# Cross attention and a routed feed-forward layer on one core: token groups with the residual added on TensorE, the weight work moved

## What is computed

```python
q  = layernorm(x) @ Wq.T + bq            # then scores over the 64 keys
x  = x + softmax(q @ (ctx @ Wk.T).T * D**-0.5) @ (ctx @ Wv.T + bv) @ Wo.T + bo
xt = layernorm(x)
p, idx = top_k(softmax(xt @ Wr + br), 2);  p = p / p.sum()
h  = layernorm(relu(xt @ W1[e] + b1[e])) * g1[e] + be1[e]     # 128 -> 512
y  = layernorm(relu(h @ W2[e] + b2[e])) * g2[e] + be2[e]      # 512 -> 128
out = x + sum over the token's 2 experts of p * y
```

## Time and profile before

| | us |
|---|---|
| median of 3 runs | 352.91 (352.75 to 356.93) |
| profiled execution, its own time | 354.07 |
| span of its trace | 352.3 |
| busy: DVE, PE, ACT, POOL | 274.4 (78%), 226.2 (64%), 214.7 (61%), 172.8 (49%) |

### The profile page before, as it was taken

How to read it: one execution, slowest core, us unless ns; L and a number is a source line. 1 busy time by engine, 2 the same in 40 slices (tenths; PEclk the granted TensorE clock), 3 DMA queues, 4 the chain that set the end, 5 groups by cost and what they waited for, 6 DMA issues and landing times.

```text
span 352.3 us, 10394 instructions
## 1 busy us (share of the span) xinstructions
PE 226.2 (64%) x2809; PEld 188.6 (54%) x2809; DVE 274.4 (78%) x1263; ACT 214.7 (61%) x715; POOL 172.8 (49%) x265
## 2 busy tenths in 40 slices
PE   2960394956281402000299999999999989996900
PEld 2640343444141301000299999999999979982300
DVE  1885066548697987896069999999999989995396
ACT  2631092925446637231169999999999979984243
POOL 9001917443544736457005666666666656665000
PEclk9995558585555555555599999999999999996555
DMA  7798801110101101013121222222222222211964
GB/s 196 232 297 199 241 3 53 32 38 16 45 23 38 39 31 53 23 38 105 47 62 41 72 70 72 64 77 65 78 69 71 71 64 64 73 39 38 339 227 150
DMA packets 31278, 31.31 MB, mean 89 GB/s; under 512 B 5027, under 2 KB 23811, under 8 KB 31220
## 3 DMA queue, kind: packets, MB, share of 16 engines
q1 hardware_dynamic: 23716, 19.46, 19.9%
q0 software_dynamic: 4320, 8.89, 8.1%
q10 hardware_dynamic: 3184, 2.30, 2.0%
HBM read 18.66 MB, written 11.97 MB: 87 GB/s over the span
## 4 chain that ended last, share of the span: by engine, by line
PE 44%; DVE 25%; SPq 10%; issue 9%; another core or an unknown queue 3%; POOL 3%; DMA 3%; ACT 1%; DVEq 0%; ACTq 0%; POOLq 0%
PE bank L523 22%; PE bank L527 20%; SPq L393 4%; SPq L386 3%; PE bank L708 2%; POOL slot_rows L498 2%; DVE w2f L1270 2%; DVE x L1132 2%; DVE topi L1189 2%; DVE w2l L1276 2%; DVE w1l L1281 2%; DVE st L1139 1%; DVE w1f L1498 1%; DMA gb<-in_L_ffn_be 1%
## 5 line engine op out<-in xcount | busy, mean ns | idle before, releaser
L498 POOL DMA_INDIRECT slot_rows<-pay,pos x64 | 63.3, 990 | 61.0 <-DVE pos L1227 36.3
L510 POOL DMA_INDIRECT answers<-vo,xs x71 | 73.8, 1040 | 29.1 <-ACT sd L980 26.3
L523 PE MATMUL bank<-xsT,w1h 128*128 128x128 f16 x568 | 56.3, 221 | 0.7 <-issue 0.5
L1421 DVE SCALAR_TENSOR_TENSOR kb<-bank,rh 128x512 f16<-128x512 f32 x71 | 47.9, 675 | 10.9 <-ACT rh L966 10.8
L523 PE MATMUL bank<-xsT,w1l 128*128 128x128 f16 x284 | 52.2, 221 | 0.0
L527 PE MATMUL bank<-rh 128*128 128x129 f16 x284 | 51.5, 220 | 0.0
L527 PE MATMUL bank<-w2h,rh 128*128 x284 | 51.4, 219 | 0.0
L527 PE MATMUL bank<-w2l,rh 128*128 x284 | 51.4, 219 | 0.0
L966 ACT ACTIVATE rh<-bank 128x512 f16<-128x512 f32 x71 | 42.4, 597 | 14.4 <-PE bank L523 9.1
L523 PEld LDWEIGHTS bank<-xsT,w1h 128*128 x568 | 43.1, 99 | 3.6 <-issue 1.5
L527 PE MATMUL bank<-w2h,kb 128*128 x284 | 39.7, 220 | 1.3 <-DVE kb L1421 1.3
(11 more groups left out here) (212 smaller groups left out, 624.1 us busy)
## 6 DMA issues: line engine op xcount, KB each, us to landing
xs<-slot_rows SPq DMA_DIRECT2D x71, 64.5 KB
x_tok<-in_x SPq DMA_DIRECT2D x16, 128.0 KB, 3.0
w1f<-in_L_ffn_W SPq DMA_DIRECT2D x2, 1024.0 KB, 7.1
w1f<-answers SPq DMA_DIRECT2D x4, 512.0 KB, 5.1
w2f<-answers SPq DMA_DIRECT2D x4, 512.0 KB, 8.9
answers<-vo,xs POOLq DMA_INDIRECT x71
w2h<-in_L_ffn_W SPq DMA_DIRECT2D x4, 256.0 KB, 8.7
w2l<-in_L_ffn_W SPq DMA_DIRECT2D x4, 256.0 KB, 12.8
```

Source lines behind the costliest of these rows:

```text
L498: eng.indirect_dma_start(slots, bass.IndirectOffsetOnAxis(ap=pos[:, g % 2, k, i:i + 1], axis=0), pay[g % 2][:, k, i, :], None).then_inc(s_ ...
L510: eng.indirect_dma_start(answers, bass.IndirectOffsetOnAxis(ap=xs[j % NX][:, 2 * D:2 * D + 2].bitcast(U32), axis=0), z[j % NZ], None).then ...
L523: return eng.matmul(dst, lhsT, rhs, start=start, stop=stop)
L1421: eng.scalar_tensor_tensor(out=rl[j % 2][:, :, :], in0=psH[j % 3][:, :].rearrange("p (c n) -> p c n", c=FC), scalar=0.0, in1=rh_all(j), op ...
```

## The change

- x is loaded in 8 pieces with 1 KB runs; `w1_last` goes to ACT's DMA queue, g1, be1 and b2 are loaded ahead of W2, half of x behind W1.
- The residual and its router product are added by PE in the attention's PSUM bank (`skip`, 4 products of 136 columns); ACT copies the sum out (`x2_copy`) in place of DVE's `x2_`.
- The key bias enters PSUM as a product (8 or 24 rows by 256 columns) of the standard deviations' transpose and a table that POOL makes with 16 selects; DVE takes the maximum from PSUM, ACT's exponential scales by rstd. The probabilities are divided by their sum on DVE before the transpose.
- The root's guess is one exponential of the bits on ACT, then two Newton steps on DVE (6 steps for 12).
- Ranks are summed in PSUM over the groups (`base`, `ranks`, `base_next`); DVE's rank, count and cast instructions go.
- The copy of the payload is a DMA on SP instead of an ACT instruction.
- Orders: PE transposes x for group n+2 behind the ranks of group n-1, not ahead of the scores; ACT copies that transpose ahead of `xt`. Square sums go to passes 2 to 4 in quarters, centring to passes 4 to 7, the high parts to 6 to 8, and of the low parts 14 of 16 behind `tables`.

```diff
-        CENTRE = {3: (0, 1), 4: (2, 3), 5: (4, 5), 6: (6, 7)}
-        UP_LO = {5: (0,), 6: (1, 2), 7: (3, 4), 8: (5, 6, 7)}
-        DOWN_LO = {5: (0,), 6: (1, 2), 7: (3, 4), 8: (5, 6, 7)}
+        CENTRE = {4: (0, 1), 5: (2, 3), 6: (4, 5), 7: (6, 7)}
+        UP_LO = {7: (0, 1), 8: (2, 3, 4, 5, 6, 7)}
+        DOWN_LO = {8: range(8)}
...
+            for g in range(GROUPS):
+                eng.wait_ge(s_lo, g + 1)
+                eng.dma_start(pay[g % 2][:, 1, :, 0:2 * D], pay[g % 2][:, 0, :, 0:2 * D]).then_inc(s_copy[g % 2], 16)
...
+                mm(bank[1][:, 0:GT * KEYS], sdT[n][:, :],
+                   kb_tile[n][:, g * GT - first:(g + 1) * GT - first, :].rearrange("p i k -> p (i k)"), stop=False)
...
+            def skip(g):
+                if g >= 1:
+                    eng.wait_ge(s_x2, g)
                 for i in range(GT):
+                    mm_beside(attn(i // 2, i % 2), xT[g % 2][:, i * P:(i + 1) * P], ident_wr[:, :], i % 2 == 0)
...
+            def base_next(g):
+                m = mask[g % 2]
+                eng.wait_ge(s_pos, g + 1)
+                mm_beside(base, not_below[:, :], m[:, :])
+                for d in range(1, GT):
+                    t = mm_beside(base[:, 0:(GT - d) * E], onesb[:, :], m[:, d * E:])
...
+            def root_guess(v, y_, sem):
+                eng.activation(y_, v.bitcast(U32), ACT.Exp, bias=guess0[:, 0:1], scale=-0.5 * LN2 / (1 << MANTISSA)
+                               ).then_inc(sem, 1)
...
+            for e_ in range(E):
+                eng.dma_start(w1_last[e_], A["L0_ffn_W1"][e_, D - 1:D, :].to_broadcast([P, F])).then_inc(ld_w1_last, 16)
...
             tables()
+            for e_ in UP_LO[GROUPS]:
+                w_up_lo(e_)
+            for e_ in DOWN_LO[GROUPS]:
+                w_down_lo(e_)
             gate_diff()
             gates()
```

More of the change, by code:

```diff
@@ L163, in build @@
         oh = sb("oh", [P, GROUPS, K, GT, E])
-        mask = sb("mask", [P, GT, E], BF16)
-        filled = sb("filled", [P, 2, E])
-        rank = sb("rank", [P, GT, E])
-        pick = sb("pick", [P, K, GT, E])
-        posf = sb("posf", [P, K, GT])
+        mask = [sb(f"mask{n}", [P, GT * E], BF16) for n in range(2)]
+        pick = sb("pick", [P, K, GT * E])
         pos = sb("pos", [P, 2, K, GT], U32)
@@ L481, in gpsimd @@
                               channel_multiplier=0).then_inc(s_const, 1)
+            for n in range(2):
+                c, first = (FIRST, 0) if n == 0 else (TILES - FIRST, FIRST)
+                from_act(eng, f"key_bias{n}")
+                for b in range(c // 2):
+                    of_tile = kb[0:c, first // 2 + b:first // 2 + b + 1, :].to_broadcast([c, 2, KEYS])
+                    t = eng.affine_select(out=kb_tile[n][:, 2 * b:2 * b + 2, :], in_=of_tile, compare_op=ALU.is_equal,
+                                          fill=0.0, base=-2 * b, pattern=[[-1, 2], [0, KEYS]], channel_multiplier=1)
+                t.then_inc(s_sel, 1)
             eng.wait_ge(ld_w1_last, 16 * E)
@@ L603, in totals, with w_rows @@
                 mm(bank[6][:, 0:2 * FC + 1], ones[:, :], ss[:, :]).then_inc(p_tot, 1)
-            def w_rows(h):
-                eng.wait_ge(ld_b2, 16)
-                eng.wait_ge(s_gm, 1)
-                eng.wait_ge(ld_w2[h], 16)
-                mm(bank[6 + h][0:2, :], second[:, :], half(b2row, h), stop=False)
-                for n in range(h * H * FC, (h + 1) * H * FC):
+            def w_rows(h, part):
+                first = h * H * FC
+                if part == 0:
+                    eng.wait_ge(ld_b2, 16)
+                    eng.wait_ge(s_gm, 1)
+                    eng.wait_ge(ld_w2[h], 16)
+                    from_act(eng, "values2")
+                    mm(bank[6 + h][0:2, :], second[:, :], half(b2row, h), stop=False)
+                for n in range(first + part * H * FC // 2, first + (part + 1) * H * FC // 2):
                     at_d = (n // FC) % H * D
@@ L1093, in stats1, with newton @@
                 stat.up(t)
-            def root1_(first, end):
-                tiles = slice(first * GT, end * GT)
-                eng.wait_ge(q_stat, stat.n)
-                for k in range(12):
-                    root_step(k, 0, mv1a[:, tiles, 1], tiles, root1)
-            def bias_(g):
+            def newton(k, v, y_, yy, vyy, z, r):
+                a = y_ if k < 3 else z
+                if k % 3 == 0:
+                    return eng.tensor_tensor(yy, a, a, ALU.mult)
+                if k % 3 == 1:
+                    return eng.scalar_tensor_tensor(out=vyy, in0=yy, scalar=-0.5, in1=v, op0=ALU.mult, op1=ALU.mult)
+                return eng.scalar_tensor_tensor(out=z if k == 2 else r, in0=vyy, scalar=1.5, in1=a, op0=ALU.add,
+                                                op1=ALU.mult)
```

670 lines of the change are left out of this document (364 added, 306 removed).

## The result

| | kernel before | changed kernel |
|---|---|---|
| median of 4 runs, us | 353.33 (352.75 to 356.93) | 361.2 (359.63 to 364.1) |
| ratio, 95% interval | | 1.021 (1.011 to 1.031) |
| profiled execution: its time, span | 354.07, 352.3 | 359.9, 358.0 |

The change makes the kernel some 2% slower; the interval leaves out no change and reaches from 1 to 3%. I had forecast 341, 3% faster, with a range of 330 to 352: wrong in the direction, and outside the range.

What follows compares the result with a forecast made beforehand. It took the experts as bound by PE and the group loop by DVE and its waits. 19.7 us gained in the groups less 8.0 lost before the experts gave -11.7, so 341 us, range 330 to 352.

Steps and rivals of the forecast that it cites:

- The gain in the groups: Group loop: the last row numbers would end at 137.3 us against 157.0, 19.7 gained.
- two corrections nearly cancel: Group passes: +4 us for DVE stops without a cause, -4 for PE running part of the time at full clock.
- the clock's 4: Passes 1 to 5: PE's higher granted clock would save a third of 5 x 2.4 us, so -4.
- the gain is taken back: Rival: unexplained DVE and ACT stops fall on the new chain (+7), gains land at 33.7 (+2.2); 350 us, chance 0.25.
- The start: Start of the group loop: group 1's maximum would start at about 31.5 us.
- The road over the gains: Start: g1 and be1 load behind 4.5 MB on SP's queue, landing at 31 us, from 26 to 33.7.
- The chain over the transposes of x: Passes 1 to 5: ranks, transposes of x, ACT's copy, `xt`, payload follow in turn; 13.6 us in pass 2.
- The tail: From the last row numbers to the experts' first product: 25.5 us against 17.5, 8.0 lost.
- register loads of PE: Tail: PE's 11 register loads come after the gates, 0.5 us each, 5.5 in all (from 0 to 5.5).
- first turn to first product: Last term of the tail, before the experts: 1.45 us.
- The scatters end inside it: Tail: the last scatters (10.1 us and some 6 to the first rows) would end within its 25.5 us.
- Experts: Experts' loop and tail, from the first product to the end: unchanged at 177.8 us.

Runs made afterwards that it cites:

- the second profile of the same kernel: The kernel before, unaltered, run again where the follow-up experiments ran: 338.48 us, span 336.7.
- the pair without stops: The kernel before and the changed kernel, both unaltered, run again where the follow-up experiments ran: 338.48 and 344.4 us, ratio 1.0225.
- the kernel with waits: The changed kernel with DVE waiting for each of its 14 low parts before it starts the next: 344.39 us, ratio 1.018 to the kernel before.
- the control: The changed kernel, unaltered, run again where the kernel before takes 338 us: 344.4 us, ratio 1.0225.

## Why the prediction was wrong, point by point

**The gain in the groups: -19.7 forecast, -5.5 measured; the largest error.** I set the row numbers of the changed kernel, added up from parts (137.3), against those of the kernel before as its trace had them (157.0). That trace held 14.0 us of stops that the second profile of the same kernel does not have. The step that failed is the price of these stops in the sum of parts: the 4 us of "two corrections nearly cancel", which I had from the one row at 111.8 us, where the changed kernel's profile held 12.4 (114.2 less 101.7). So both sides carry the stops, and I took most of them off one. The rest of the passes is as I had it: 101.7 measured without stops, 101.8 from the parts (105.8 less the clock's 4, most of which came in one pass at nearly full clock).

Without stops on either side my own terms give 31.5 + 101.8 = 133.3 against 141.9, 8.6 gained, less 8.0 lost in the tail: 0.6 us faster, that is no change. So the stops made a gain of 3% out of nothing, and the slower kernel comes from the two terms that follow. In the pair without stops the spans differ by 3.8 us and the medians by some 6: the start took 5.3 us more than forecast and the tail lost 9.4 for 8.0, while the experts gave 2.3 back. The rival "the gain is taken back" named the stops, at 7 us and a chance of 0.25.

**The start: 31.5 forecast, 37.3 measured.** The road over the gains was near in size (their transpose starts at 32.5), but for another reason: PE's value products end there, and the gains, by their issues and the times to landing, had landed by 29. The term that is missing is 4.7 us of DVE's step behind POOL's subtractions. ACT's first copy came at 11.1 and not at 9.7; the run with `w1_last` on SP's queue shows that undoing this gives 0.5 us at group 1's maximum.

**The chain over the transposes of x.** Right, and now shown by undoing it: it costs 9.5 us of the groups and some 11 to 13 of the time. I had forecast it and yet not seen that it is the change's largest single loss, because I added it to a pass that I believed to be 2 us shorter than the one before anyway.

**The tail: 25.5 forecast, 28.7 measured.** By its terms: low parts 9.7 forecast, 9.3 measured; row numbers to the end of the gates 18.6 forecast, 18.8 measured; register loads of PE 5.5 forecast, 7.5 measured (170.3 to 177.8, and 7.49 from gates to PE in the kernel with waits); first turn to first product 1.45 forecast, 2.3 measured. The 7.5 of the changed kernel's own profile are the rows' as much as the loads' (next point); the kernel with waits shows the loads alone. The mis-sized term is the register load: I took 0.5 us from SP's rows, and it is 0.68 on PE and 0.60 on DVE. The last 0.9 us, between the first turn and the first product, are not the loads': the control has 0.9 us in all there, and why the first profile has 2.3 is open. The Trainium skill (DMA: Bandwidth & Descriptors, Latency and other measured facts) has about 600 ns as the floor, and I set its 6.6 us aside; the runs agree with it (7.49 us on PE and 6.64 on DVE for 11).

**The scatter.** "The scatters end inside it" was wrong in the trace, since the low parts held one up for 9.3 us, but this costs nothing of its own in the changed kernel: the rows landed for a start at 177.84, and PE would have been ready at 170.3 plus 7.5. Three roads, the low parts with the gates and PE's loads, the scatters, and DVE's loads, end within some us of each other. So in the changed kernel the edits that free one or two of them change nothing that can be measured, or cost time. With the shorter passes, PE's loads and the gates' difference moved ahead gave 4.7 us, and DVE's loads, the last, another 6.3.

**Experts: 177.8 forecast, 177.8 measured.** The exact hit is luck: in the second pair it is 177.6 and 175.3, and I don't know where the 2.3 us come from. The variants of the changed kernel have 175.0 to 176.0, but for the two in which DVE's loads stood bare (182.7 and 180.7).

Open: what the stops of 14 and 12.4 us are. They are 8.4 of the 17.4 us by which the forecast missed. No edit was aimed at them; they stood in both first profiles and in none of the fourteen later ones.

## What to carry to other kernels

Set part against part or trace against trace, never a sum of parts against a trace: stops that the program doesn't explain sit in the trace alone. Before work is moved behind the point where two engines hand over, list every road that ends there, the engines' register loads among them; freeing one of three equal roads shows nothing, and is no proof that it was not a cause. A long run of DVE or POOL instructions back to back on SBUF can lock the other out (14 on DVE did, two or three did not); a wait of an engine for its own last instruction is a cheap way to let it in (1.6 us for 14).

## What the runs showed of the hardware that I had not expected

- DVE and POOL can lock each other out over whole runs: one scatter of 9.3 to 9.8 us beside 14 low parts in all four profiles without gaps, one DVE step of 4.8 beside the last four of eight subtractions in seven of eight. The Trainium skill's rule (above) is a lock for one instruction; without a gap, these runs show it kept through 14, and the kernel before shows it not kept through two or three. With a wait between, it changes hands: at most 1.3 us for a scatter, 0.98 for a small step of DVE.
- A register load takes 0.68 us on PE and 0.60 on DVE when nothing covers it, and next to nothing (0.6 us for all 11) when each is issued behind a DVE instruction of 0.7 us.
- A new order of PE's work alone raised its granted clock over the groups from 0.58 to 0.65. With `w1_last` on SP's queue the start lost 2 us the other way: products begun 2.8 us earlier ran at 0.56 and not at 0.96.
- The same program took 353 us in one series and 338 in the others, with the difference in stops of the passes. The ratio of the two kernels was the same, 1.021 and 1.0225.
